# Routed experts of a mixture layer in three float32r products of split parts, with both parts of four experts in a ring of slots

## The reference

```python
x = x + tanh(g_xattn[0]) * attention(layernorm(x), ctx, Wq, bq, Wk, bk, Wv, bv)   # 8 heads of 16 channels, 512 positions
x = x + tanh(g_ffn[0]) * ffn(layernorm(x), ...)

def ffn(x):                                   # 4096 tokens of 512
    h = rmsnorm(x) * rms_weight
    probs = softmax(h @ router_w)             # 8 experts
    topv, topi = top_k(probs, 2); topv /= sum(topv)
    g, u = h @ w_gate[e], h @ w_up[e]         # 512 -> 256, for the two experts of a token
    moe = sum over its two e of topv_e * ((silu(g) * u) @ w_down[e])      # 256 -> 512
    shared = (silu(h @ sw_gate) * (h @ sw_up)) @ sw_down
    return moe + shared
```

## Time and profile before

| | |
|---|---|
| median of 3 runs (lowest, highest) | 1588.44 us (1588.15, 1588.87) |
| span of the profiled execution | 1525.5 us |
| what lies around the span (difference of the two) | 62.9 us |
| first and last store of values in the attention | 81.0 and 915.0 us from the span's start |
| first and last add to the output | 1113.5 and 1519.0 us |
| PE busy | 1475.7 us, 97% of the span |
| granted PE clock, mean | 0.994 |

### The profile page before, as it was taken

The page is one execution under the profiler, slowest core; times in us unless marked ns, Lnnn a source line. Parts: engine busy times, 40 slices in busy tenths (PEclk is TensorE's granted clock), DMA queues, the critical chain, the costliest instruction groups (busy, mean ns, idle before and its releaser), DMA issues.

```text
span 1525.5 us, 23419 instructions
## 1 busy us (share of the span) xinstructions
PE 1475.7 (97%) x7362; PEld 669.8 (44%) x7362; DVE 887.8 (58%) x1802; ACT 782.5 (51%) x1531; POOL 814.5 (53%) x1241
## 2 busy tenths in 40 slices
PE   5999999999999999999999999989999999999997
PEld 1233333333333333333333328767755454545443
DVE  5888888888888888888888842512221121211111
ACT  2577777777777777777777771100022222222221
POOL 6346675766757667576674443375134444444442
PEclk9999999999999999999999999999999999999999
DMA  6566667766676666765666424785345455554554
GB/s 153 128 160 168 175 167 183 180 161 162 162 177 163 168 163 162 178 170 152 165 154 167 117 92 162 248 213 121 113 76 97 85 96 88 93 91 88 92 90 61
DMA packets 159304, 215.10 MB, mean 141 GB/s; under 512 B 28162, under 2 KB 102416, under 8 KB 158160
## 3 DMA queue, kind: packets, MB, share of 16 engines
q1 hardware_dynamic: 137136, 175.78, 44.9%
q0 software_dynamic: 17952, 37.30, 14.0%
q10 hardware_dynamic: 4096, 0.53, 0.2%
HBM read 126.12 MB, written 86.91 MB: 140 GB/s over the span
## 4 chain that ended last, share of the span: by engine, by line
PE 87%; DMA 6%; DVE 2%; issue 1%; POOL 1%; ACT 1%; SPq 1%; ACTq 0%; POOLq 0%; DVEq 0%
PE bank L1140 16%; PE bank L1062 16%; PE bank L1033 14%; PE bank L1011 14%; PE bank L1160 10%; PE bank L1135 5%; PE bank L996 4%; PE bank L1038 3%; DMA arena<-ht_d 2%; PE bank L1049 2%; PE bank L1000 2%; DMA pv_d<-arena 1%; PE bank L1148 1%; DVE row_max L696 1%; PE bank L1020 1%
## 5 line engine op out<-in xcount | busy, mean ns | idle before, releaser
L696 DVE TENSOR_REDUCE row_max<-bank 128x1 f32<-128x512 f32 x1024 | 664.9, 682 | 111.6 <-PE bank L1011 102.5
L892 ACT ACTIVATE arena<-bank 128x512 f32<-128x512 f32 x1024 | 564.5, 612 | 205.5 <-PE bank L1033 194.0
L1011 PE MATMUL bank<-arena 96*128 96x512 bf16 x1024 | 392.2, 384 | 7.8 <-DVE row_max L696 5.5
L1033 PE MATMUL bank<-arena 98*128 98x512 bf16 x1024 | 387.2, 380 | 2.9 <-ACT arena L892 1.8
L1062 PE MATMUL bank<-arena 128*32 128x512 f32 x2048 | 272.7, 605 | 1.0 <-ACT arena L892 0.7
L1140 PE MATMUL bank<-arena 128*128 x568 | 255.5, 592 | 0.0
L834 DVE TENSOR_TENSOR arena<-arena,bank 128x256 f32<-128x256 f32 x103 | 43.4, 421 | 331.7 <-ACT arena L943 327.9
L943 ACT ACTIVATE arena<-bank 128x256 f32<-128x256 f32 x103 | 39.6, 384 | 378.2 <-PE bank L1140 224.9
L604 POOL DMA_INDIRECT out<-xs,ids x71 | 112.3, 1581 | 226.3 <-ACT xs L954 184.0
L1160 PE MATMUL bank<-arena 128*128 (+1 forms) x412 | 193.8, 593 | 0.9 <-ACT arena L959 0.9
L523 POOL TENSOR_TENSOR arena<-arena 128x512 bf16<-128x512 f32 x62 | 71.6, 1155 | 226.7 <-ACT arena L884 224.0
(11 more groups left out here) (122 smaller groups left out, 1252.4 us busy)
## 6 DMA issues: line engine op xcount, KB each, us to landing
arena<-parts_q SPq DMA_DIRECT2D x64, 256.0 KB, 4.8
pv_d<-arena SPq DMA_DIRECT2D x32, 512.0 KB, 6.3
parts_k<-arena SPq DMA_DIRECT2D x96, 128.0 KB
arena<-parts_k SPq DMA_DIRECT2D x32, 384.0 KB, 4.9
parts_q<-arena SPq DMA_DIRECT2D x96, 128.0 KB
arena<-in_w SPq DMA_DIRECT2D x8, 1536.0 KB, 8.9
h_d<-arena SPq DMA_DIRECT2D x33, 256.0 KB, 6.7
out<-xs SPq DMA_DIRECT2D x33, 256.0 KB, 2.5
```

The costliest lines, as they stand in the source:

```text
L696: nc.vector.reduce_max(row_max[b % 2][:, u:u + 1], m_ps[(STEPS * b + u) % M_BANKS][:], AX_X).then_inc(s_mx, 1)
L892: nc.scalar.activation(probs[group % 3][:, j, :], e_ps[n % E_BANKS][:], ACT.Exp, scale=float(DH) ** -0.5).then_inc(s_exp, 1)
L1011: nc.tensor.matmul(m_ps[n % M_BANKS][:], q_stack[b % 3][0:STACK, h, qt * P:(qt + 1) * P], k_stack[b % 3][0:STACK, h, :], start=True, stop= ...
L1033: nc.tensor.matmul(e_ps[n % E_BANKS][:], k_stack[b % 3][0:SHIFTED, h, kt * P:(kt + 1) * P], q_stack[b % 3][0:SHIFTED, h, :], start=True, s ...
```

## The change

Each weight and each activation of the routed part is now held as two parts: a high part, written with the type float32r (ACT copies and rounds), and a low part, the difference from the unrounded value, also float32r. A product is three float32r matmuls: high x high, high x low, low x high. Where a routed tile had 4 + 2 float32 matmuls of 512 columns, it has 12 + 6 float32r ones.

Both parts of eight experts don't fit, so `w_ring` holds those of four, in the place of `w_routed`. Experts 0 to 2 are loaded raw during the shared part (jobs 5, 13, 21) and split in place by ACT and DVE in jobs 8 to 10, 16 to 18 and 24 to 26. Experts 3 to 7 are split during the attention: in each of 30 turns SP loads one row of weights (256 KB), ACT makes the high part at step 15 (`staged_high`), POOL the low part (`staged_low`), and SP stores both to DRAM (2 x 256 KB) and loads the next. In the routed part SP loads both parts of an expert (2 x 1536 KB) into a slot: expert 3 as soon as SP has come to the end of its jobs, expert e of 4 to 7 once the last tile of expert e - 4 is done. The buffer for the raw rows is the shared expert's row 0, so those weights are now loaded in the last five turns (27 to 31).

In the routed part ACT now copies the turned tokens (high part) and DVE makes low parts of tokens and activations. The gathers and the adds to the output are as before.

```diff
@@ SP
+            def load_staged(k):
+                e, r = STAGED[k]
+                if k:
+                    sp.wait_ge(s_sl, k)
+                sp.dma_start(staged_raw, w_d[1 + e, :, r, :]).then_inc(s_raw, DMA)
+
+            def store_staged(k):
+                e, r = STAGED[k]
+                for part, done in enumerate((s_sh, s_sl)):
+                    sp.wait_ge(done, k + 1)
+                    sp.dma_start(split_d[e - IN_PLACE, part, :, r, :], staged[part][:].bitcast(F32)).then_inc(s_sst, DMA)
...
                 if is_b(i + X_AHEAD):
                     load_x(i + X_AHEAD)
-                if 2 <= i < 2 + W_ROWS:
-                    sp.dma_start(w_shared[:, i - 2, :], w_d[0, :, i - 2, :]).then_inc(s_wsh, DMA)
+                if 0 <= i + 2 < len(STAGED):
+                    store_staged(i + 2)
+                if 0 <= i + 3 < len(STAGED):
+                    load_staged(i + 3)
+                if B - W_ROWS < i:
+                    r = B - i
+                    if r == 2:
+                        sp.wait_ge(s_sst, 2 * DMA * len(STAGED))
+                    sp.dma_start(w_shared[:, r, :], w_d[0, :, r, :]).then_inc(s_wsh, DMA)
...
+            def replace_expert(e):
+                if e == IN_PLACE:
+                    sp.wait_ge(s_wrt, W_ROWS * IN_PLACE)
+                    sp.wait_ge(s_eid, 1)
+                    sp.wait_ge(s_sst, 2 * DMA * len(STAGED))
+                else:
+                    sp.wait_ge(s_wrt, W_ROWS * IN_PLACE + 2 * DMA * (e - IN_PLACE))
+                    last = sp.value_load(slot_end[0:1, e - SLOTS:e - SLOTS + 1], min_val=B, max_val=JOBS)
+                    sp.wait_ge(s_dn, last)
+                for part in range(2):
+                    sp.dma_start(w_ring[:, e % SLOTS, part].bitcast(F32), split_d[e - IN_PLACE, part]
+                                 ).then_inc(s_wrt, DMA)
...
-                if j in EXPERT_JOBS:
-                    load_expert(EXPERT_JOBS.index(j))
-                if j == LATE_AT:
-                    sp.wait_ge(s_eid, 1)
-                    load_expert(EXPERTS - 1)
+                if j in LOAD_AT:
+                    load_expert(LOAD_AT[j])
...
+            for e in range(IN_PLACE, EXPERTS):
+                replace_expert(e)
@@ POOL, in each turn ahead of split(i + 3, 0)
+            def staged_low(k):
+                pool.wait_ge(s_sh, k + 1)
+                if k:
+                    pool.wait_ge(s_sst, 2 * DMA * k)
+                nc.gpsimd.tensor_tensor(staged[LOW][:], staged_raw, staged[HI][:].bitcast(F32), ALU.subtract
+                                        ).then_inc(s_sl, 1)
@@ DVE
-            def take_tokens(i):
-                dve.wait_ge(s_tr, B + i + 1)
-                dve.wait_ge(s_gu, B + i - 2)
-                nc.vector.tensor_copy(h_t[(B + i) % 3].rearrange("p c n -> p (c n)"), T_PS[i % 2][:]).then_inc(s_hr, 1)
+            def placed_low(e, r):
+                dve.wait_ge(s_ph, W_ROWS * e + r + 1)
+                nc.vector.tensor_tensor(w_ring[:, e, LOW, r, :], raw_expert[:, r, :], w_ring[:, e, HI, r, :].bitcast(F32),
+                                        ALU.subtract).then_inc(s_wrt, 1)
+            def tokens_low(i):
...
+                nc.vector.tensor_tensor(lo, T_PS[i % 2][:], hi.bitcast(F32), ALU.subtract).then_inc(s_hr, 1)
+            def act_low(j):
...
+                nc.vector.tensor_tensor(lo, A_PS[:, 0:FF], hi.bitcast(F32), ALU.subtract).then_inc(s_al, 1)
@@ ACT (staged_high at step 15 of a turn; take_tokens ahead of silu)
+            def staged_high(k):
+                act_e.wait_ge(s_raw, DMA * (k + 1))
+                if k:
+                    act_e.wait_ge(s_sl, k)
+                    act_e.wait_ge(s_sst, 2 * DMA * k)
+                nc.scalar.copy(staged[HI][:], staged_raw).then_inc(s_sh, 1)
...
+            def take_tokens(i):
+                act_e.wait_ge(s_tr, B + i + 1)
+                if i >= 2:
+                    act_e.wait_ge(s_gu, B + i - 1)
+                nc.scalar.copy(h_parts[i % 2][HI][:].rearrange("p c n -> p (c n)"), T_PS[i % 2][:]).then_inc(s_hh, 1)
@@ PE
+            def three_products(out, parts, j, first_row, chunks):
+                hi, lo = parts
+                for c in range(chunks):
+                    for n, (v, part) in enumerate(((hi, 0), (hi, 1), (lo, 0))):
+                        last = nc.tensor.matmul(out, v[:, c, :], routed_weights(j, part, first_row + c),
+                                                start=(c == 0 and n == 0), stop=(c == chunks - 1 and n == 2))
+                return last
...
-                    if j == B:
-                        pe.wait_ge(s_wrt, EXPERTS * DMA)
+                    pe.wait_ge(s_wrt, expert[j][1])
...
-                    for c in range(CHUNKS):
-                        last = nc.tensor.matmul(G_PS[j % 2][:], h_t[j % 3][:, c, :], routed_weights(j, c),
-                                                start=(c == 0), stop=(c == CHUNKS - 1))
+                    last = three_products(G_PS[j % 2][:], h_parts[(j - B) % 2], j, 0, CHUNKS)
```

More of the change, by code:

```diff
@@ L9 @@
 BF16 = mybir.dt.bfloat16
+F32R = mybir.dt.float32r
 ALU = mybir.AluOpType
@@ L68 @@
 X_AHEAD = 7
+SLOTS = 4
+IN_PLACE = SLOTS - 1
+STAGE_AT = 15
 class Arena:
@@ L295, in build @@
         JOBS = B + NT
-        EXPERT_JOBS = range(5, 5 + 2 * (EXPERTS - 1), 2)
+        STAGED = [(e, r) for e in range(IN_PLACE, EXPERTS) for r in range(W_ROWS)]
+        PLACED_JOBS = {5: range(8, 11), 13: range(16, 19), 21: range(24, 27)}
+        LOAD_AT = {j: e for e, j in enumerate(PLACED_JOBS)}
+        PLACED_AT = {j: [(e, 2 * n), (e, 2 * n + 1)]
+                     for e, jobs in enumerate(PLACED_JOBS.values()) for n, j in enumerate(jobs)}
         EXP_AT = 6
         COUNT_AT = 8
-        LATE_AT = EXPERT_JOBS.stop
         MAP_AT = B - 4
@@ L858, in _ @@
                     next(pieces, None)
+                for e, r in PLACED_AT.get(j, ()):
+                    placed_low(e, r)
                 if j == TURN_AT:
@@ L972, in _ @@
                     weigh(j - B - 1)
+                for e, r in PLACED_AT.get(j, ()):
+                    placed_high(e, r)
         @block.tensor
@@ L1157, in down @@
                         pe.wait_ge(s_yrt, j - 1 - B)
-                for f in range(FF // P):
-                    w = w_shared[:, CHUNKS + f, :] if j < B else routed_weights(j, CHUNKS + f)
-                    last = nc.tensor.matmul(Y_PS[j % 2][:], act_t[j % 2][:, f, :], w,
-                                            start=(f == 0), stop=(f == FF // P - 1))
+                if j < B:
+                    for f in range(FF // P):
+                        last = nc.tensor.matmul(Y_PS[j % 2][:], act_t[j % 2][:, f, :], w_shared[:, CHUNKS + f, :],
+                                                start=(f == 0), stop=(f == FF // P - 1))
+                else:
+                    last = three_products(Y_PS[j % 2][:], act_parts[j % 2], j, CHUNKS, FF // P)
                 last.then_inc(s_dn, 1)
```

82 lines of the change are left out of this document (69 added, 13 removed).

## The result

The changed kernel takes 1645.07 us (median of 4 runs, 1642.05 to 1651.56), the kernel before on the same chip 1588.65 (1588.15 to 1596.51). The ratio is 1.035, with a 95% interval of [1.0319, 1.0381]: slower by 56 us, where 9 were forecast, and above the range of 1566 to 1632.

A forecast was written before the change was run, and what follows sets the result against it. PE was taken to bound the kernel, with the chain of adds just behind. -18.3 - 2 + 15 + 19 - 5 = +8.7 us, with 62.9 us around the span unchanged, gave 1597 us; range 1566 to 1632.

The forecast's parts named there:

- The main step: Routed part: PE falls to 4.5 us a tile with float32r at 0.22 us, so the 5.53 us chain of adds decides.
- The shared part and first tiles: Five of eight expert loads leave the shared part, -5 us; the first two tiles run at PE's pace, 2 us earlier.
- the slot loads, +15: Routed part: five 3 MB loads beside the adds delay them 4 us each, the first mostly ahead of them; +15 us.
- the gain of 18.3 us: Routed part: the 70 intervals between adds shrink from 405.4 us to 387.1, at 5.53 each.
- the attention: +17 forecast: Attention: three 256 KB transfers a turn in SP's queue cost 0.6 us in each of 28 turns.
- the first turns: Start of the attention, where PE waits on transfers one by one: a load and two stores more, +2 us.
- some 1.0 is covered: Attention: of DVE's 1.75 us wait a turn for the sums, 1.0 costs nothing and about 0.75 lengthens the turn.
- The trial in the earlier trace: Attention, turns 2 to 7: one 256 KB transfer there added 0.43 us of wait, 0.13 of turn; scaled to three.
- The upper end given for that term, 45: Attention: no room after the first transfer, 0.8 us for each further one, 28 x 1.6 = 45 us.
- what lies around the span: Outside the profiled span of 1525.5 us: 62.9 us up to the median of 1588.4, said to stay.
- Rival 4: Heavier taxes: load packets hold the adds (+40), a turn loses 1.3 us or more (+36); 1625 to 1645 us, chance 0.12.
- 2 in 10: Chance stated for outcomes outside the range of 1566 to 1632 us.

The follow-up runs named there:

- 7: Changed kernel with one float32r product (high x high) in place of three, on a chip without the hole: 1579.47 us, ratio 1.0377 to the kernel before.
- 5: Changed kernel without the attention's transfers of split weights except the first load; ACT's and POOL's splitting stays; chip without the hole: 1542.0 us, ratio 1.0131.
- after: The changed kernel as first measured and profiled, against the kernel before: 1645.07 us, ratio 1.035; profiled span 1644.0 us.
- run 4: Changed kernel with the attention's transfers of split weights moved behind the store of tokens, ahead of the stores of k: 1635.31 us, ratio 1.0272.
- 3: Changed kernel without the slot loads of experts 4 to 7, expert 3's load kept: 1634.78 us, ratio 1.0269.
- 6: Changed kernel with all transfers of split weights in the attention, but splitting done for the first row only; chip without the hole: 1586.64 us, ratio 1.0424.
- 8: The changed kernel again, no edit, on a chip with the hole: 1643.37 us, ratio 1.0324.
- second profile of before: The kernel before profiled again, no edit, on a chip with the hole: 1591.88 us, ratio 1.0011; profiled span 1589.0 us.
- the spans without the map: Changed kernel and kernel before, each without the 64 indirect writes of the map of places: 1577.78 and 1516.25 us; profiled spans 1571.5 and 1516.2 us.

## Why the prediction was wrong

**Right.** The main step: PE's time a tile falls below the 5.53 us of the adds (4.8 measured), the adds become the floor (7), and PE's saving of some 70 us is not seen in the time. Float32r went at 0.23 us. The shared part and first tiles gave back 4 of 7. ACT's and POOL's splitting costs nothing (5).

**Near in size, not in form: the slot loads, +15.** The four loads behind expert 3's cost 15 us beside after and 22 beside run 4, and expert 3's, which was put at nothing, 3 more. They cost it by four waits of 6.4 us, where 3 to 4 were forecast. The waits add up to 25.6; that only 15 come on top beside after has to do with its shorter steady intervals, whose cause is open. That 15 was met is partly luck.

**Wrong, the gain of 18.3 us.** The step "the 70 intervals are 405.4 us, and at 5.53 they are 387.1" took the floor of a steady interval as the mean of all. Without the four slot loads they take 404.9, or 402 without expert 3's share too: a gain of 3 at most. Part of this stood in the trace of before: four of its intervals, the 15th, 22nd, 37th and 54th, are 6.3 to 6.9 us long, and the same four are long in 3 (6.5 to 7.3). Before, such lateness was made good: the 70 intervals take 405.4 in spite of it, less than 70 times PE's 5.82 (407.4). Now each us of it ends in the chain. Of the eleven longer intervals in 3, some end with `weigh`, some with the add before, some with nothing that the profile names; their cause is open.

**Wrong, the attention: +17 forecast, +40 measured** (and +4.5 for the first turns in place of +2). That the cost is the three transfers' and not ACT's or POOL's is shown by 5 and 6. The wait itself was forecast nearly right: +1.3 a turn, and (67.8 - 22.8) / 32 = 1.4 came. What failed is "some 1.0 is covered": most of the extra wait is not. In the runs, DVE's extra wait against before's 22.8 and the attention's extra length against 834.2 go together:

| run | extra wait, us | extra length, us |
|---|---|---|
| 5 no transfers | -3 | -1 |
| 4 moved | +25 | +27 |
| 6 transfers alone | +42 | +36 |
| after again (8) | +40 | +36 |
| 7 one product | +39 | +29 |
| after | +45 | +40 |

So 0.7 to 1.1 us of length come with each us of extra wait; that the length comes by this wait, and not by something else that the transfers delay, is argued from this table and from PE's longer wait for the maxima, and no run sets the wait alone. The trial in the earlier trace rows could not carry the proportion: it gave 0.13 us of turn for 0.43 of wait, 0.8 us over six turns, and in the second profile of before the same six turns take 27.28 us against 27.22, with a wait of 0.60 against 0.47. One transfer costs next to nothing, three cost 1.4 us a turn (28.63 over the turns of the earlier trace rows, where 27.8 was forecast). The upper end given for that term, 45, is close to what came.

**Wrong, what lies around the span.** The 62.9 us do not exist: 1.7 us lie there. The rest was a hole of some 70 us in the shared part, which the profiled execution of before did not have and its median did. As both kernels have it on such chips, the difference hardly suffers: ratios of 1.032 to 1.035 there, and 55.3 us between the spans without the map. The changed kernel itself never ran on the other kind of chip; run 6, which is nearly it, shows 1.042 there. But the largest loss of the kernel was booked as something no change can touch.

In sum, 8.7 + 18 (adds) + 25.6 (attention and its first turns) + 2.7 (shared part) = 55. Rival 4 had the attention's tax (+36) and nearly the total (1625 to 1645), with a chance of 0.12, but by luck: its +40 for the slot loads is about twice what they cost, and it kept the gain of 18 that did not come. The chances left outside the range add up to 0.26, not to the "2 in 10" of the text.

## What to carry to other kernels

When the bound moves from an engine to a chain of dependent transfers, take the mean of that chain over the whole stretch, not its steady interval: here the engine that bounded hid the chain's lateness, and the chain hid none of its own. An extra wait of an in-order engine in a tightly coupled loop is to be priced nearly in full unless a run shows cover (here 0.7 to 1.1 of it). Large loads beside a chain of small transfers are worth trying in pieces, each after the last has landed (here 20 us). And if span and median differ by more than a few us, the profile is of another case than the median.

## What the runs showed that was not expected

- Beside 64 indirect writes of 128 rows of 8 bytes, one each 1.26 us, TensorE gets only one matmul each 0.7 to 2.8 us on some chips, for some 70 us, and not on others; the writes move 0.06 MB in that time. By what way, and why chips differ, is open.
- A float32r matmul of 512 columns takes 0.23 us, as a bf16 one.
- A chained indirect add of 256 KB rises from 4.7 to 11.4 us of landing beside two transfers of 1536 KB, which bring one packet of some 10.5 KB for each of its own of 2 KB; in pieces with rows of 2 KB the same bytes leave it at 5.9 at most.
